# A graph attention layer with routed experts: two semaphores for each slot of the gather ring, and a wait at every gather

## What is computed

```python
x = x + gnn(_layernorm(x), ...)
x = x + experts(_layernorm(x), ...)

# gnn, heads H = 4, OUT = 64
ft = (feat @ W).reshape(n, H, OUT)
e = e_src[src] + e_dst[dst]            # leaky relu, then softmax over the edges of each dst
a = ex / denom[dst] * dist
m = ft[src] * a                        # one row of ft fetched for each edge
out = jax.ops.segment_sum(m, dst, num_segments=n)
```

## Time and profile before

| | |
|---|---|
| median of 3 runs | 3641.94 us (3638.27 to 3663.85) |
| the profiled execution's own time | 3680.23 us, its span 3678.5 us |
| first gather of the main stage starts | 242.47 us |
| last gather of the main stage starts | 2793.74 us |
| GpSimd busy | 2102.3 us, 57% |
| TensorE busy (matmuls) | 2334.5 us, 63% |
| VectorE busy | 1944.0 us, 53% |
| ScalarE busy | 1505.3 us, 41% |
| bytes moved | 394.55 MB, mean 107 GB/s |
| mean granted TensorE clock | 0.802 |

### The profile page before, as it was taken

One profiled execution on the slowest core, in us unless ns is written; L12 is line 12 of the kernel. 1 busy time (PEld: TensorE's weight loads), 2 busy tenths in 40 slices (PEclk: granted clock), 3 DMA queues, 4 the chain that ended last, 5 costly groups with the idle time before them and its releaser, 6 DMA issues. The chain is left out here.

```text
span 3678.5 us, 53462 instructions
## 1 busy us (share of the span) xinstructions
PE 2334.5 (63%) x10832; PEld 1847.1 (50%) x10833; DVE 1944.0 (53%) x4409; ACT 1505.3 (41%) x2731; POOL 2102.3 (57%) x2068
## 2 busy tenths in 40 slices
PE   5734455555555555555665656656656689999995
PEld 4523333434434444444544545444445578777774
DVE  5443343444555556556666666666666843333332
ACT  5612222233334334344444445444445345444442
POOL 0026666666666666666656555555541467777775
PEclk9856776777777777777777878777777799999998
DMA  5423444444444444444444444444432424545453
GB/s 163 158 74 108 108 108 105 116 115 109 118 115 123 117 124 115 125 124 127 121 130 122 130 116 123 121 113 115 118 108 61 70 57 79 81 78 82 80 81 50
DMA packets 231558, 394.55 MB, mean 107 GB/s; under 512 B 55832, under 2 KB 148796, under 8 KB 230881
## 3 DMA queue, kind: packets, MB, share of 16 engines
q0 software_dynamic: 114816, 265.53, 30.8%
q1 hardware_dynamic: 76728, 89.16, 9.0%
q10 hardware_dynamic: 39924, 38.86, 3.2%
HBM read 325.36 MB, written 69.42 MB: 107 GB/s over the span
## 5 line engine op out<-in xcount | busy, mean ns | idle before, releaser
L1001 POOL DMA_INDIRECT m_rows<-table,src_col x1568 | 1507.0, 961 | 1085.9 <-issue 480.8
L1387 PE MATMUL m_A<-m_msg,m_by_edge 128*128 128x260 f32 x3920 | 1297.7, 500 | 516.1 <-issue 391.6
L1387 PEld LDWEIGHTS m_A<-m_msg,m_by_edge 128*128 128x128 f32 x3920 | 976.8, 256 | 751.5 <-issue 537.0
L1245 ACT ACTIVATE m_apart<-m_drow,nid 128x1024 bf16 x297 | 341.1, 1148 | 949.0 <-SPq L969 887.2
L1085 DVE TENSOR_TENSOR m_msg<-m_rows,m_A 128x2048 f32<-128x2048 f32 (+1 forms) x294 | 568.2, 1933 | 104.0 <-issue 85.8
L1053 DVE TENSOR_REDUCE m_e_sum<-m_E 128x64 f32<-128x192 f32 x295 | 105.0, 356 | 649.4 <-PE m_E L1373 317.1
L1373 PE MATMUL m_E<-m_look_parts,m_by_node 128*128 x2368 | 109.3, 177 | 519.9 <-ACT m_by_node L1248 494.7
L1373 PEld LDWEIGHTS m_E<-m_look_parts,m_by_node 128*128 128x128 bf16 x2368 | 97.9, 100 | 602.6 <-issue 577.2
L1593 POOL DMA_INDIRECT out<-x_con,x_to_i x206 | 329.4, 1599 | 107.1 <-issue 70.1
L1248 ACT ACTIVATE m_by_node<-m_apart,m_one 128x1024 bf16<-128x1024 bf16 x297 | 341.1, 1149 | 9.7
L1046 DVE TENSOR_TENSOR m_by_edge<-m_A,row 128x1024 f32<-128x1024 f32 (+1 forms) x295 | 307.3, 1042 | 30.6 <-issue 25.1
(11 more groups left out here) (249 smaller groups left out, 2400.7 us busy)
## 6 DMA issues: line engine op xcount, KB each, us to landing
m_drow<-dst_row SPq DMA_DIRECT2D x196, 256.0 KB
m_rows<-table,src_col POOLq DMA_INDIRECT x1568
table<-f_rowbuf SPq DMA_DIRECT2D x14, 924.0 KB, 4.9
ydram<-m_y ACTq DMA_DIRECT2D x49, 264.0 KB
m_xb<-in_x ACTq DMA_DIRECT2D x48, 256.0 KB
out<-m_x ACTq DMA_DIRECT2D x48, 256.0 KB
f_xin<-in_x SPq DMA_DIRECT2D x13, 896.0 KB, 6.9
x_w<-in_L_ffn_expert_w SPq DMA_DIRECT2D x18, 256.0 KB, 6.0
```

Source lines behind the costliest of these rows:

```text
L1001: nc.gpsimd.indirect_dma_start(rows[:, g % RING, j, :], None, table, bass.IndirectOffsetOnAxis(ap=K.src_col[:, g, j:j + 1], axis=0)).then_ ...
L1245: a.activation(apart[i][:, :], drow[:, bass.ds(g % RING, 1), :].rearrange("p a n -> p (a n)"), ACT.Abs, bias=K.nid[:, bass.ds(b, 1)], scal ...
L1387: m = t.matmul(psA[i][:, 0:ROW], by_edge[i][:, j, :], msg[i][:, j, :], start=(j == tiles[0]), stop=(j == tiles[-1]))
```

## The change

Each slot gets two semaphores in place of one: the even gathers of a group count on `gathered[0][slot]`, the odd ones on `gathered[1][slot]`. GpSimd no longer stops once a group until the group before has landed; instead it waits at every gather for the landing of the one two places ahead of it, over the group boundary too. So at most two gathers are under way at a time. `slot_free` is waited for as before. SyncE's `announce` waits for both semaphores of the slot, and the waits at the end are doubled in the same way.

```diff
+FLIGHT = 2
-        gathered = [sem(f"gathered{i}") for i in range(RING)]
+        gathered = [[sem(f"gathered{f}_{i}") for i in range(RING)] for f in range(FLIGHT)]
             def announce(c, i):
 
-                sp.wait_ge(gathered[i], 16 * GT * (c + 1))
+                for f in range(FLIGHT):
+                    sp.wait_ge(gathered[f][i], 16 * (GT // FLIGHT) * (c + 1))
         @block.gpsimd
         def _(pool):
+            def landed(n):
+
+                pool.wait_ge(gathered[n % FLIGHT][n // GT % RING],
+                             16 * (n // GT // RING * (GT // FLIGHT) + n % GT // FLIGHT + 1))
+
             def gather(g):
                 for j in range(GT):
+                    if g or j >= FLIGHT:
+                        landed(g * GT + j - FLIGHT)
                     nc.gpsimd.indirect_dma_start(
                         rows[:, g % RING, j, :], None, table,
-                        bass.IndirectOffsetOnAxis(ap=K.src_col[:, g, j:j + 1], axis=0)).then_inc(gathered[g % RING], 16)
+                        bass.IndirectOffsetOnAxis(ap=K.src_col[:, g, j:j + 1], axis=0))\
+                      .then_inc(gathered[j % FLIGHT][g % RING], 16)
 
             for g in range(NG):
                 if g >= RING:
                     pool.wait_ge(slot_free, g - RING + 1)
-                if g:
-                    pool.wait_ge(gathered[(g - 1) % RING], 16 * GT * ((g - 1) // RING + 1))
                 gather(g)
-            for i in range(RING):
-                pool.wait_ge(gathered[i], 16 * GT * NCH)
+            for f in range(FLIGHT):
+                for i in range(RING):
+                    pool.wait_ge(gathered[f][i], 16 * (GT // FLIGHT) * NCH)
```

## The result

| | before | changed |
|---|---|---|
| median | 3648.48 us (3638.27 to 3663.85, 4 runs) | 3785.49 us (3782.43 to 3789.25, 4 runs) |
| ratio of times | | 1.037, 95% interval 1.033 to 1.0415 |
| the profiled execution, its span | 3680.23 us, 3678.5 us | 3782.43 us, 3780.7 us |
| mean granted TensorE clock | 0.802 | 0.783 |

The change costs 137 us by the medians and 102 us between the two profiled executions. The forecast was 189 us more, 3831 us. The sign, the place of the loss and the range held; the size was too large by this comparison.

The account below looks back on a forecast made before the run. Gathers were taken to bound the kernel through group 139, fading until 168; 176 + 10 + 3 + 0 = 189 us, added to the median 3641.9, gave 3831 us, 5.2% slower, range 3740 to 3920.

Parts of the forecast that it names:

- The bound: Main stage: GpSimd's gathers set the pace in groups 0 to 139, at 12.55 us each; this fades until group 168.
- The stop taken apart: GpSimd's stop once a group: 2.13 us from a gather's end to the waiting start, about 0.45 more for a separate wait.
- rival A: Gathers: landing gets quicker when at most two are under way; 12.09 us a group, 3577 us; chance 3%.
- Two chains at 3.09 us: GpSimd's even and odd gathers: each starts 0.96 + 2.13 = 3.09 us after the one two ahead.
- 12.81 + 0.65 + 0.35 = 13.81 us a group: Early groups: 12.81 us for the slower chain, 0.65 for the spread's delay, 0.35 for ScalarE's traffic.
- B: Rival: spread and ScalarE's traffic don't delay gather landings; group 12.81 us, 3678 us in all; chance 10%.
- C: Rival: every gather's wait costs like the separate one, 2.58 us; group 15.16 us, 4068 us in all; chance 5%.
- Groups 140 to 167: Stretch where the effect fades: 10 us more for groups 140 to 153, 3 us for groups 154 to 167.
- SyncE's second wait: SyncE's announcement of a group: waiting for two semaphores adds zero; without cover, under 0.1 us.
- The last 28 groups: nothing: Groups 168 to 195, about 15 us each, already slower than 13.81, so the change adds nothing.
- first term: Groups 0 to 139: 140 x (13.81 - 12.55) = 176 us more.
- D: Rival: late groups pay too, as consumers' slack shrinks, with contention at upper bounds; 299 us more, 3941 us; chance 12%.

Follow-up runs that it names:

- e10_one: The changed kernel with one gather under way, each waiting for the landing of the one just ahead: 6117.5 us (1 run).
- e11_swap_before: The kernel before with its two waits ahead of a group exchanged, so the gather carries the landing wait: 3452.8 us, ratio 0.969.
- e8_no_stop: The kernel before without the wait for the landing of the group before; slot_free still waited for: 3168.2 us, ratio 0.888.
- e7_thin_before: The kernel before with the spread cut from 256 KB to 2 KB from group 4 on: 3565.2 us (1 run).
- e1_swap_after: The changed kernel with the two waits at each group's first gather exchanged, so slot_free is the separate wait: 3758.4 us, ratio 1.0535.
- e12_thin_swap: The changed kernel with both the spread cut to 2 KB and the two waits at each group's first gather exchanged: 3608.2 us (1 run).
- e4_thin_after: The changed kernel with the spread cut from 256 KB to 2 KB from group 4 on: 3669.5 us (1 run).
- e5_before_again: The kernel before, unchanged, profiled once more on a later occasion: 3568.0 us (10 runs).
- e9_four: The changed kernel with four semaphores in turn, each gather waiting for the one four ahead: 3165.4 us, ratio 0.8885.

## Why the prediction was right, and where its sizes were off

**The bound.** Right. Gathers set the pace to group 140 and beyond; everything that changed them changed the time (e10_one, e11_swap_before, e8_no_stop), and what left them alone did not (e7_thin_before).

**The stop taken apart.** Right to 0.06 us. From the three early stops I had 2.13 us from the end of a gather to the start of one that waits for it, and 0.45 us more for the separate wait. The packets give 1.48 + 0.60 = 2.08 us, and 1.48 + 1.11 = 2.59 with the separate wait. e10_one and e11_swap_before show both prices alone. The page "DMA: Bandwidth & Descriptors" of the Trainium skill, section "Anatomy of one DMA — SWDGE (gpsimd) path", by which I had estimated 2.31 us, is 0.2 us above the 2.09 us from the end of the descriptors to the next start with one gather alone in e10_one. Its section "Latency and other measured facts", the ground of rival A, has a lighter load make the fixed cost smaller; nothing of that showed in e10_one, where the idle time was the same with one gather in flight.

**Two chains at 3.09 us.** Right: 3.04 to 3.06 us where nothing disturbs them.

**12.81 + 0.65 + 0.35 = 13.81 us a group.** It took 13.58. The step that failed is "it delays the one on the slower chain": I put the separate wait and the spread on the same chain and added them. The spread's delay was sized well (0.60 measured between 12.98 and 13.58, 0.65 taken), but it falls mostly on the second gather, which is odd, while the separate wait is on the first, which is even. A gather starts after the later of the two chains, so the one delay hides under the other: the separate wait is worth 0.05 us beside the spread (e1_swap_after), 0.27 without it (e12_thin_swap), and 0.45 in my sum. The pace that nothing disturbs was 0.20 us too high as well: 12.36 is 4 x 3.09, and the measured 3.04 give 12.16. With both delays gone e12_thin_swap takes 12.71, so 0.55 us are left for ScalarE's traffic and whatever else is beside the gathers, within the bounds of 0 and 0.60 that I had set but not the 0.35 that I took; no run takes that traffic alone. Taken off in this order the parts are 12.16 + 0.55 + 0.27 + 0.60 = 13.58 us, against 12.36 + 0.35 + 0.45 + 0.65 = 13.81. That the first two errors cancel is luck. Over 140 groups the 0.23 us are 32 of the 176 us. B, that the transfers beside cost nothing, is wrong by the 0.60 us of e4_thin_after, and C, a dear wait at every gather, by the 3.04 us of e10_one.

**Groups 140 to 167.** 13 us expected, 9 measured (145 to 154 us behind). Against the undisturbed profile of before, e5_before_again, it is 34 (148 to 182).

**SyncE's second wait.** Zero, as said: e9_four has four waits in `announce` and one at each gather, and is as fast as e8_no_stop.

**The last 28 groups: nothing.** This failed, by 52 us between the two profiles. I took their 15 us a group for a property of the kernel that the change leaves alone. It was one of that execution: on the later occasion the same kernel took 12.6 to 12.7 us for them (342 us for 27). In the first profile the changed kernel gained there, 13.8 against 15.3 us; on the later occasion it lost, 14.0 against 12.7. The forecast's sum was made against one execution whose end was slower than the kernel needs, with register instructions of VectorE and ScalarE of which over 300 took some 0.70 us, where no other profile has one over 0.25, and which show in no row of the views. The step that failed is "the last 28 groups, slower than 13.81 already, nothing". Had I taken the 12.53 us of a gather-bound group as the floor for the end too, the sum would have been larger, not smaller: on the later occasion the change costs 213 us, above the 189, and on the first 137. So the forecast lies between the two by luck: against the undisturbed before its first term was too large (176 us, measured 148) and its other two too small (13 and 0 us, measured 34 and 40). D, that late groups pay as well, thus came true there, for another reason than the one given: the late groups were not bound by the consumers for good.

**The range.** From its stated contention of 0.35 to 1.6 us a group the same sum gives 3728 to 3932 us, and not 3740 to 3920. The result lies inside either.

**What stays open.** Why VectorE's and ScalarE's register instructions were slow in the first profile of before, and how much of the 69 us from group 168 to 195 they account for: they took 38 and 15 us more there, partly at the same time, and no run isolates them. The granted clock was lower too (0.76 against 0.83), and the longer matmuls are another 20 us. That the clock fell because TensorE idled while it waited for the slower engines would fit, and so would the highest mean clock, 0.849, in e8_no_stop, where TensorE's share of busy time is the largest; it is not shown.

## What to carry to other kernels

Work out the pace of a chain of waited-for transfers from three numbers of the trace: descriptor writing (here 1.26 us a gather with the step), end to landing (1.48), landing to the next start (0.60). With n in flight a gather took the larger of 1.26 us and 3.04/n here, for n of 1, 2 and 4 and without what delays landings, so two in flight (13.58 us a group with its delays) lose even to eight with a full stop (12.53), and four cost nothing (10.14); a stop that is spread out over every gather is not removed but paid where all small delays are on the path. Look also at which of two waits at one instruction is split off: if it is the one that comes last, exchange them (110 us here for two lines). And before a sum leans on how a stretch behaves, read the same stretch in a second execution, register instructions included.

## What was not expected of the hardware

- The same program, 3648 us on one occasion and 3562 to 3568 on three others, with its first 140 groups equal to 3 us in the profiles, and what follows 111 us apart (1679.0 and 1567.8 us from group 140 to the end). In the slower profile 258 register instructions of VectorE and 70 of ScalarE in the main stage took some 0.70 us each; in the other 13 profiles none of these two engines took over 0.25.
- A separate wait instruction ahead of a gather costs 0.5 us only when its event is the late one: 1.11 against 0.60 us from landing to start. It was 1.07 to 1.44 us at each of 191 places in both profiles of the changed kernel, in e4_thin_after, in e5_before_again and in e7_thin_before.
- A 256 KB transfer, 0.97 us of all engines' time by the estimate from the earlier trace rows, delays the landing of the gather that it meets by 0.9 us on average, and by 1.3 at group 93 (2.77 in place of 1.48 us). In e8_no_stop landings were as late, up to 3.0 us in groups 84 to 97, and GpSimd did not wait for them.
